# Typed messages: gathered rows stream past a standing one-hot, their sums pass through ScalarE and a TensorE transpose, and the loop is 14 supertiles long

## What is computed

```python
def _L1_gnn_ref(h, weight, norm, src, dst, rel_type):
    transformed = jnp.einsum('ni,rio->rno', h, weight)      # 16 relations
    msg = transformed[rel_type, src] * norm
    return jax.ops.segment_sum(msg, dst, num_segments=h.shape[0])

def _L1_mix_ref(x, Wq, Wkv, Wproj, bproj):
    q = elu(x @ Wq.T) + 1; k = elu(...) + 1                 # 8 heads
    context = einsum('bhnd,bhne->bhde', k, v)
    attn = einsum('bhnd,bhde->bhne', q, context) * D_inv
    return attn @ Wproj.T + bproj
```

## Time and profile before

| | us |
|---|---|
| median of 3 runs | 4316.6 (4314.61 to 4317.24) |
| span of the profiled execution | 4536.6 |
| of it, up to the relations stage | 2425.7 |
| of it, the relations stage (line 819's first row to line 811's) | 1159.4 |
| of it, all that follows | 951.5 |

### The profile page before, as it was taken

The page is one execution under the profiler, slowest core; times in us unless marked ns, Lnnn a source line. Parts: engine busy times, 40 slices in busy tenths (PEclk is TensorE's granted clock), DMA queues, the critical chain, the costliest instruction groups (busy, mean ns, idle before and its releaser), DMA issues. The chain is left out here.

```text
span 4536.6 us, 87874 instructions
## 1 busy us (share of the span) xinstructions
PE 3879.2 (86%) x23793; PEld 3488.4 (77%) x23793; DVE 2970.3 (65%) x6850; ACT 2025.5 (45%) x4761; POOL 2146.1 (47%) x2102
## 2 busy tenths in 40 slices
PE   7899999999999987998996567756676669999996
PEld 6798898989898877996885556655666658888885
DVE  7698999989898887555332123223232359999898
ACT  3465556656565546773221000000000148888784
POOL 0355555555555511000004666666666347877773
PEclk9899999999999997999996566566555579999997
DMA  4466666656565620004443333333333123332225
GB/s 137 131 175 172 173 171 173 176 170 176 170 176 170 171 68 23 19 8 148 154 149 119 89 91 92 88 90 90 88 90 91 46 69 73 71 76 68 67 49 130
DMA packets 227003, 509.12 MB, mean 112 GB/s; under 512 B 51806, under 2 KB 94300, under 8 KB 220427
## 3 DMA queue, kind: packets, MB, share of 16 engines
q0 software_dynamic: 116736, 313.66, 24.9%
q1 hardware_dynamic: 106389, 187.30, 14.6%
q10 hardware_dynamic: 3679, 5.79, 0.4%
HBM read 434.08 MB, written 72.49 MB: 112 GB/s over the span
## 5 line engine op out<-in xcount | busy, mean ns | idle before, releaser
L686 POOL DMA_INDIRECT big<-table,e_idx x784 | 750.9, 958 | 1040.5 <-DVE e_idx L722 647.6
L357 POOL DMA_INDIRECT big<-table,e_idx x784 | 766.2, 977 | 857.3 <-issue 293.1
L704 PE MATMUL psum<-e_near_hot,big 128*128 128x64 f32 x3136 | 639.5, 380 | 372.9 <-issue 361.3
L704 PEld LDWEIGHTS psum<-e_near_hot,big 128*128 128x128 f32 x3136 | 633.0, 300 | 389.1 <-issue 386.4
L2202 POOL DMA_INDIRECT g_S<-gsrc,g_idx x512 | 610.9, 1193 | 219.0 <-issue 164.3
L749 DVE TENSOR_TENSOR big<-big,psum 128x128 f32 x196 | 56.7, 289 | 809.9 <-remote 475.2
L469 DVE TENSOR_TENSOR big<-psum,big 128x512 f32<-128x512 f32 x784 | 539.5, 688 | 47.2 <-PE psum L369 15.8
L436 ACT ACTIVATE e_hT_hi<-psum 128x256 fp32r<-128x256 f32 x784 | 300.3, 383 | 591.2 <-PE psum L376 504.8
L387 PE MATMUL psum<-e_w_hi,e_hT_hi 128*128 128x256 f32 x1568 | 509.8, 325 | 0.1
L387 PE MATMUL psum<-e_w_hi,e_hT_lo 128*128 128x256 f32 x1568 | 443.8, 283 | 0.0
L387 PE MATMUL psum<-e_w_lo,e_hT_hi 128*128 128x256 f32 x1568 | 440.4, 281 | 0.0
(11 more groups left out here) (416 smaller groups left out, 9018.0 us busy)
## 6 DMA issues: line engine op xcount, KB each, us to landing
big<-in_attr_t SPq DMA_DIRECT2D x392, 128.0 KB
g_rest<-gpart SPq DMA_DIRECT2D x128, 256.0 KB
big<-table,e_idx POOLq DMA_INDIRECT x1568
table<-C SPq DMA_DIRECT2D x26, 896.0 KB
table<-n_rows SPq DMA_DIRECT2D x24, 896.0 KB
experts<-g_region SPq DMA_DIRECT2D x15, 560.0 KB
g_S<-gsrc,g_idx POOLq DMA_INDIRECT x512
table<-big SPq DMA_DIRECT2D x25, 224.0 KB
```

What stands on the lines that cost most here:

```text
L357: pool.indirect_dma_start(G[:, j % 2, q, :], None, table, bass.IndirectOffsetOnAxis(idx[:, j, q:q + 1], 0)).then_inc(s[f"G_in{j % 2}{q}"], 16)
L686: pool.indirect_dma_start(G[:, j % n, q, :], None, c.table1, bass.IndirectOffsetOnAxis(idx[:, j, q:q + 1], 0)).then_inc(s[f"G_in{j % n}"], 16)
L704: last = pe.matmul(acc[:, b, :], G[:, j % n, q, b * 128:(b + 1) * 128], onehot[:, q, :], start=q == 0 and (b == 0 or s is sems[1]), stop=q ...
```

## The change

In `stage_relations` the operands of the sums swap roles. Now the weighted one-hot (128 edges x 64 nodes) stands, and the gathered rows move, all 256 features at once: 4 matmuls a supertile instead of 8, and the sums come out with 64 nodes on the partitions. ACT copies them to a small SBUF tile (`sums_kept`, two buffers), PE transposes them in two steps of 128 x 64 into another PSUM bank, and DVE adds that to `agg` as before, but two supertiles later instead of one. The sums use banks 4 and 5, the turned sums banks 6 and 7.

The loop is 14 supertiles long with one attention turn, and has 12 rounds. The turns are 12 of 261 nodes each, so `CT` has 7 columns more than there are nodes, filled with zeros. `TURN` becomes 7, so the row numbers come in halves of 7 supertiles, and DVE writes them one supertile later than before (at 1 and 8 of the 14).

```diff
@@ stage_relations
-    SUPS = 28
+    SUPS = 14
     NB = NSUP // SUPS
     TURN = SUPS // 2
     NEAR_SLOTS, FAR_SLOTS, ACCS = 7, 2, 4
+        sums_kept = sb("sums_kept", [WIN, 2, D])
...
+            def summed(a, beside):
+                k, j, sup = a
+                _, onehot, _ = window(sems[0], j)
+                pe.wait_ge(sems[0]["hot_ready"], sup + 1)
+                pe.wait_ge(sems[0][f"G_in{j % n}"], (k * (SUPS // n) + j // n + 1) * 16 * SUP)
+                pe.wait_ge(kept, sup + 1)
+                for q in range(SUP):
+                    last = pe.matmul(near_sums(j), onehot[:, q, :], G[:, j % n, q, :], start=q == 0, stop=q == SUP - 1)
+                    if q == SUP - 1:
+                        last.then_inc(sems[0]["sup_done"], 1)
+                    if beside and q == 0:
+                        beside()
+            def turn(a):
+                k, j, sup = a
+                _, _, acc = window(sems[0], j)
+                pe.wait_ge(kept, sup + 1 + 2)
+                pe.wait_ge(sems[0]["added"], sup + ACCS - 1)
+                pe.sem_inc(begun_turning, 1)
+                for b in range(KB):
+                    last = pe.transpose(acc[:, b, :], sums_kept[:, j % 2, b * 128:(b + 1) * 128], c.ident[0:WIN, 0:WIN])
+                last.then_inc(turned, 1)
+            def step(k, v, beside=None):
+                a = at(k, v)
+                if a:
+                    summed(a, beside)
+                a = at(k, v - 1)
+                if a:
+                    turn(a)
...
+                    act.wait_ge(sems[0]["sup_done"], sup + 1 + NEAR_SLOTS)
+                    act.wait_ge(turned, sup + 1)
+                    act.activation(sums_kept[:, j % 2, :], near_sums(j), ACT.Copy).then_inc(kept, 1)
...
             def add_window(a):
                 k, j, sup = a
-                dve.wait_ge(s["sup_done"], p * NSUP + sup + 1 + NEAR_SLOTS)
+                if s is sems[0]:
+                    dve.wait_ge(turned, sup + 1 + 2)
+                else:
+                    dve.wait_ge(s["sup_done"], p * NSUP + sup + 1 + NEAR_SLOTS)
...
-                a = at(k, v - 1)
+                a = at(k, v - (2 if s is sems[0] else 1))
                 if a:
                     add_window(a)
                 a = at(k, v)
-                if a and a[1] == 0:
+                if a and a[1] == 1:
                     if not (isinstance(a[0], int) and a[0] == 0):
                         indices(a[0], 1)
-                elif a and a[1] == TURN and not (isinstance(a[0], int) and a[0] == NB - 1):
+                elif a and a[1] == TURN + 1 and not (isinstance(a[0], int) and a[0] == NB - 1):
                     indices(a[0] + 1, 0)
...
             @block.scalar
             def _(act):
+                act.activation(c.CT[:, :, NODES:PADDED], c.ones[:, 0:1].unsqueeze(2).broadcast_to([128, KB, PADDED - NODES]), ACT.Copy,
+                               scale=0.0).then_inc(padded, 1)
...
-                attention.on_scalar(act)
+                act.sem_inc(kept, 2)
+                act_near(act)
```

More of the change, by code:

```diff
@@ L668, in whole @@
                     step(0, v)
-                with eng.Fori(0, NT // GROUP) as g:
+                with eng.Fori(0, Attention.TURNS) as i:
                     for v in range(SUPS):
-                        step(g + 1, v, lambda: aside(eng, v % TURN, g, v // TURN, (g + 1) * SUPS + v))
-                for v in range(SUPS + 1):
+                        step(i + 1, v, lambda: aside(eng, v, i, (i + 1) * SUPS + v))
+                for v in range(SUPS + 2):
                     step(NB - 1, v)
@@ L688, in pool_pass, with pe_near, aside @@
                             s[f"G_in{j % n}"], 16)
-        def pe_pass(pe, s, p):
+        def pe_near(pe):
+            n = NEAR_SLOTS
+            def summed(a, beside):
[26 more added lines that the diff above has]
+                    turn(a)
+            def aside(pe, w, i, sup):
+                if w in Attention.PE_STEPS:
+                    attention.on_tensor(pe, Attention.PE_STEPS[w], i)
+            loop_beside(step, 0, aside)(pe)
@@ new lines, in act_near, with step, aside @@
+        def act_near(act):
+            def step(k, v, beside=None):
+                a = at(k, v)
+                if a:
+                    k, j, sup = a
+                    act.wait_ge(sems[0]["sup_done"], sup + 1 + NEAR_SLOTS)
+                    act.wait_ge(turned, sup + 1)
+                    act.activation(sums_kept[:, j % 2, :], near_sums(j), ACT.Copy).then_inc(kept, 1)
+                if beside:
+                    beside()
+            def aside(act, w, i, sup):
+                if w == Attention.ACT_STEP:
+                    attention.on_scalar(act, i)
+            loop_beside(step, 0, aside)(act)
@@ L691, in pe_pass, with pe_far, step @@
+        def pe_far(pe, s, p):
             n = slots(s)
[L693 removed]
+            def step(k, v):
                 a = at(k, v)
@@ L704, in step, with pe_pass @@
                         last = pe.matmul(acc[:, b, :], G[:, j % n, q, b * 128:(b + 1) * 128], onehot[:, q, :],
[L705 removed]
+                                         start=q == 0, stop=q == SUP - 1, skip_group_check=True)
                     if q == SUP - 1:
                         last.then_inc(s["sup_done"], 1)
[L708 to L714 removed]
+            loop(step, 0)(pe)
+        def pe_pass(pe, s, p):
+            if s is sems[0]:
+                pe_near(pe)
+            else:
+                pe_far(pe, s, p)
         def dve_pass(dve, s, p):
```

57 lines of the change are left out of this document (28 added, 29 removed).

## The result

The changed kernel takes 4325.2 us in the median of 7 runs (4320.3 to 4329.3), the kernel before 4312.4 in 7 runs beside them (4308.1 to 4317.2): a ratio of 1.0026, 95% interval 1.0017 to 1.0036. That is 12.7 us more, small, but outside the 0.2% within which I had called it no change.

The account below looks back on a forecast made before the run. POOL's gathers were taken to bound the relations stage, with other stages packed. Terms summed to 0, give or take 2 us; 2 us for a warmer clock gave 4314 us. The 8-in-10 range was 4205 to 4350, the forecast's own 4308 to 4322.

Parts of the forecast that it names:

- What bounds the stage: Relations stage: POOL's gathers, one every 1.25 us, set its pace in timed runs; PE is quicker.
- The weaker rival: Relations stage: POOL's 0.30 us gaps are the profiler's, PE sets 4.8; full clock gives 4306 to 4217; faster rivals together 0.32.
- Do the stalls exist without the profiler?: Relations stage: PE's stalls, 170 us in the profiled execution, are gone or nearly gone in timed runs.
- the subtraction: Median 4316.6 us less other stages' profiled 3377.2 leaves 939 us for the relations stage, 4.8 a supertile.
- Sums, transposes, copy: Relations stage, PE and ACT: sums 3.1 to 3.4 us, transposes 0.2 to 0.45, copy 0.38, all hidden: 0.
- May hold the higher level: PE's clock in the relations stage: wide sums may keep it at the higher level; no gain while gathers hide them.
- End of the stage: Relations stage, after the last sums: copy, transposes and hand-overs +1.1 us, warmer clock -1.6; net -1 to +1.5.
- 2 us for a warmer clock: Start of the stage after relations: a warmer PE clock saves 2 us.
- Loop and attention: Relations stage: 13 POOL loop ends instead of 6, and 12 attention turns instead of 10, cost 0.
- The rivals: Relations stage: stalls or PE's time real, so faster, chance 0.32; late row numbers or PE over POOL's pace, slower, 0.18.
- Slower: Relations stage: late row numbers, +33 us to 4350, or PE's path passing 4.8 us, +20 per 0.1 us; chance 0.18.
- Row numbers: Relations stage: DVE writes them later, so POOL waits some 2.5 us a round if PE lags six supertiles: +33 us.

Follow-up runs that it names:

- loops alone: Kernel before with loops of 14 supertiles and 12 attention turns of 261 nodes, old sums in two PSUM banks: 4318.6 us, ratio 1.0013.
- sums alone: Kernel before with the new sums, ACT copy and PE transposes, in loops of 28 supertiles with 10 turns: 4317.85 us, ratio 1.0012.
- form alone: Kernel before with four wide matmuls a supertile, without copy and transposes, so results are wrongly arranged: 4317.7 us, ratio 1.0013.
- before, short one-hots: Kernel before with a supertile's four one-hots made by four short DVE instructions in place of two: 4308.45 us, ratio 0.9990.
- changed, short one-hots: Changed kernel with a supertile's four one-hots made by four short DVE instructions: 4316.7 us, ratio 1.0007.
- the same, code put back: Changed kernel with four short one-hot instructions and 3356 never executed ones, so PE's later code lies where it lay before: 4309.7 us, ratio 0.9991.
- before, code moved: Kernel before with 228 never executed PE instructions, placing its later code as in the changed kernel modulo 32768 bytes: 4314.9 us, ratio 1.0006.
- The kernel with the loops and short one-hots: Kernel before with loops of 14 supertiles, twelve attention turns and four short one-hot instructions, old sums: 4310.8 us, ratio 0.9989.
- the changed kernel with three gathers: Changed kernel with three gathers a supertile instead of four, all sums still on PE: 4082.2 us.
- the sums' part with them: Kernel before with the changed sums in loops of 28 supertiles and four short one-hot instructions: 4309.8 us, ratio 0.9986.

## Why the prediction was wrong, point by point

A table of the stages first, from the profiles on chips without stalls (us; "late" is the lateness, "tail" runs from the last gather's start to the stage's end, "next" the time from the stage's end to the graph attention's first gather, "rounds" that from its first to its last `g_spread`):

| kernel | relations | late | tail | next | rounds | ratio of the timed runs |
|---|---|---|---|---|---|---|
| before | 994.7 | 5.8 | 9.0 | 69.1 | 770.6 | 1 |
| changed | 1000.3 | 9.7 | 10.7 | 66.2 | 776.9 | 1.0026 |
| loops alone | 997.6 | 8.3 | 9.3 | 70.5 | 770.5 | 1.0013 |
| sums alone | 1000.5 | 9.5 | 11.1 | 67.3 | 770.7 | 1.0012 |
| form alone | 1000.4 | 11.3 | 9.2 | 65.7 | 768.7 | 1.0013 |
| before, short one-hots | 989.5 | 0.5 | 9.0 | 69.7 | 769.6 | 0.9990 |
| changed, short one-hots | 992.6 | 1.9 | 10.8 | 65.6 | 777.2 | 1.0007 |
| the same, code put back | 991.4 | 0.4 | 11.1 | 66.4 | 770.7 | 0.9991 |
| before, code moved | 994.7 | 5.3 | 9.5 | 69.7 | 775.6 | 1.0006 |

- **What bounds the stage** was right: POOL's gathers, 1.25 us apart. Taking a gather of four away took 244.5 us of the stage in both kernels. The weaker rival is out with it: the 0.30 us behind each gather stand in profiles that are as long as the timed runs, so they aren't the profiler's.
- **"Do the stalls exist without the profiler?"** The answer for the timed runs shown, no, was right; its reason was wrong. I put the stalls down to the profiler being on; a second profile has none, and one chip has such stalls in its timed runs as well. The numbers drawn from the subtraction fell with it. I held the other stages at their profiled length since they looked packed; in the second profile the part ahead of the stage is 35.5 us shorter (2390.4 against 2425.9) and the part behind it 23 us. So the stage is 995 us in an undisturbed run and not 939, and the pace 5.0 us a supertile and not 4.8. The range went down to 4205 on the strength of stalls that can't be won; nothing was won of them.
- **Sums, transposes, copy.** Sizes about right: 3.60 us of sums near half clock (0.53) where I had 3.1 to 3.4, a pair of transposes 0.30 to 0.33 (0.2 to 0.45), a copy 0.377 (0.38). "May hold the higher level" came true (0.82). That the cost is 0 was the step that failed: I asked only who waits for whom, by semaphores. POOL's gathers wait for DVE's one-hots without one. The change moved DVE's one-hots against the gathers, which cost 3.9 us more of lateness (9.7 against 5.8). The first trace had it: 59 of its 784 gathers take over 1.0 us, and I never put them beside the one-hots.
- **End of the stage.** I gave between -1 and +1.5 net, +1.1 if the sums stay at half clock. They did stay near it at the end (3.60 us for the last eight records); the tail grew by 1.7 us, above my range. 1.4 us of it are the longer way: DVE starts the last addition 2.3 us behind the end of PE's last sum, and 0.9 us in the second profile of the kernel before. The other 0.4 us lie ahead of the last sums (4.4 us behind the last gather's start, 4.0 before). Before, and in the changed kernel:

```profile
3380.10 3.65 PE L704 MATMUL psum<-e_near_hot,big 128*128 128x64 f32 x16 [2.53 <-issue]
```

```profile
3384.66 0.29 DVE L749 TENSOR_TENSOR big<-big,psum 128x128 f32 x1 [5.89 <-PE psum L704]
```

```profile
3382.03 3.60 PE L707 MATMUL psum<-big,e_near_hot 128*64 128x256 f32 x8 [2.83 <-issue]
...
3386.19 0.30 PE L720 MATMUL psum<-ident,e_sums_kept 64*128 64x64 f32 x2 [0.29 <-ACT e_sums_kept L743]
```

```profile
3387.92 0.29 DVE L814 TENSOR_TENSOR big<-big,psum 128x128 f32 x1 [0.85 <-DVE big L814]
```

- **2 us for a warmer clock** behind the stage: 69.1 against 66.2 us to the graph attention's first gather, 2.9, with a granted clock of 0.55 against 0.63 on the way. The size is right, but that the wide sums bring it is not shown. The kernel with the loops and short one-hots has the old sums, a clock of 0.50 in its last 10 us, and 65.3 us; the changed kernel with three gathers has wide sums, 0.77 there, and 70.5 us.
- **Loop and attention** at 0: no row shows a cost at POOL's loop ends or of turns in other numbers. What failed is that I asked what the loop's code costs in its own stage, and put the stages behind it at nothing without a reason. I had the rule that seems to matter in my hands and used it on one engine in one stage. The Trainium skill's Runtime: NRT & Kernel Launch, "Instruction fetch mechanics", says that a taken branch to code not held has to wait for it. The trace of this case fits it in a place that I didn't look at: PE, at a few loop rounds of a later stage, 6.3 us in all.
- **The rivals.** Slower came true, but by none of the mechanisms named. Row numbers were never late: POOL's wait for `e_idx` is 645.5 us in the changed kernel and 646.1 in the kernel before, all of it ahead of the first gather. PE's path never passed POOL's pace.
- **The number.** 4314 stood on 4316.6 us for the kernel before, the median of three runs; seven have 4312.4. Against that I had forecast 2 us less and 12.7 more came. The 4325.2 lie above the forecast's own 4308 to 4322, by less than they would without that start. They do lie inside 4205 to 4350, but the reasons that I gave for either end didn't come up, so that is luck.

The parts, as the profiles have them: 3.9 late gathers + 6.3 code + 1.7 tail - 2.9 start of the next stage = 9.0 us. The late gathers and the tail leave 5.6 for the stage (1000.3 against 994.7). The spans of the two profiles differ by 7.4 us, the stages ahead and behind having moved by 1.6 the other way. The timed difference is 12.7 (7.3 to 15.5), so 3.7 us of it have no place in this sum, which its interval covers. By the timed runs, short one-hots bring the changed kernel from 1.0026 to 1.0007, putting the code back to 0.9991, and there it stands beside the kernel before with short one-hots at 0.9990: nothing is left over that these runs can tell (each ratio is known to 0.0009, 4 us). That each part alone came to half the total looks like chance: their shares are late gathers, the tail and the spread of 4 us in either ratio, and the code's 6 us appear in neither.

The version to keep is the kernel before with the four short one-hots, 0.1% faster than before (the sums' part with them, 0.9986, can't be told from it); the changed kernel needs them and 3356 instructions that never run to get as far.

## What to carry to other kernels

When a change is priced at zero because it lies beside the bounding engine's work, look also at what two engines share without a semaphore (here whatever lets a one-hot of DVE hold a gather of POOL) and at the code behind the changed place, which moves. Compare all stages of two traces, not only the one that was edited: half of this loss lay where the diff has no line. And when a profile is longer than the timed runs, take a second one, best on another chip, before explaining the difference.

## What was unexpected on the chip

- One chip runs this program 290 us (6.7%) slower than the four others named in the runs, at nearly the same granted clock in its packed stages (0.99 against 1.00 in the first layer's messages), with PE falling behind by 10 to 20 us every four or five supertiles of the relations stage. Other stages are slower as well (1485 against 1445 us in the first layer's gathers).
- A gather of 128 rows of 1 KB takes POOL 0.946 us, and up to 1.2 us in the changed kernel (1.3 with the form alone) when it meets a DVE instruction that reads two tensors of SBUF: it then ends 0.82 us behind that instruction's end. `tensor_scalar` with two columns of scalars, a quarter as wide, follows the same rule and costs a gather 0.08 us at most; a reciprocal costs it nothing.
- 64-column sums at 32 bits left PE's clock at 0.60 over the stage; the same sums with 256 columns moving raised it to 0.82, and to 0.94 where POOL feeds them a third faster.
- 14592 bytes of never executed code cost 5 us in loops far behind them.
